# A fused LayerNorm, mLSTM and spiking-FFN kernel: linked small normalisation steps split up, fewer of them, and new instruction orders

## What is computed

```python
q = layernorm(x)
ig, fg = gates(q, c, c)                      # 8 input and 8 forget gates per token
D = exp(cumsum(log_sigmoid(fg)) differences + ig - row maximum), lower triangle
C = (q k^T / sqrt(32)) * D
h = C / (max(|C.sum(-1)|, exp(-rowmax)) + 1e-6) @ v
x1 = x + tanh(g_xattn) * layernorm(h) * ln_scale
y = square(relu(layernorm(x1) @ W_fc^T)) @ W_proj^T
out = x1 + tanh(g_ffn) * (spikes of 5 integrate-and-fire steps driven by y) / 5
```

## Time and profile before

| | |
|---|---|
| median of 3 runs | 615.34 us (615.02 to 616.83) |
| profiled execution, span | 615.3 us |
| TensorE busy | 571.4 us (93%), 6032 matmuls |
| VectorE | 526.3 us (86%), 1291 instructions |
| GpSimd | 493.3 us (80%) |
| ScalarE | 485.8 us (79%) |
| mean granted TensorE clock | 0.980 |

### The profile page before, as it was taken

How to read it: one execution, slowest core, us unless ns; L and a number is a source line. 1 busy time by engine, 2 the same in 40 slices (tenths; PEclk the granted TensorE clock), 3 DMA queues, 4 the chain that set the end, 5 groups by cost and what they waited for, 6 DMA issues and landing times.

```text
span 615.3 us, 17747 instructions
## 1 busy us (share of the span) xinstructions
PE 571.4 (93%) x6032; PEld 479.2 (78%) x6032; DVE 526.3 (86%) x1291; ACT 485.8 (79%) x1011; POOL 493.3 (80%) x541
## 2 busy tenths in 40 slices
PE   0568988999999999999999999999999999999995
PEld 0357888887888888888788888888888888887894
DVE  4789889989989898989989898989999888878446
ACT  3776878897888888888888788888888777776673
POOL 4878889996997889887997889887997887955542
PEclk9995989999999999999999999999999999999998
DMA  8775736664664637662663637752675427401002
GB/s 271 168 145 115 160 74 124 168 139 95 124 149 96 155 84 127 171 146 70 123 163 83 158 83 131 187 126 70 121 167 130 87 48 148 121 4 35 0 2 70
DMA packets 73193, 71.34 MB, mean 116 GB/s; under 512 B 8720, under 2 KB 68752, under 8 KB 73104
## 3 DMA queue, kind: packets, MB, share of 16 engines
q1 hardware_dynamic: 71888, 70.00, 50.5%
q10 hardware_dynamic: 1216, 0.21, 0.2%
HBM read 27.44 MB, written 8.39 MB: 58 GB/s over the span
## 4 chain that ended last, share of the span: by engine, by line
PE 82%; SPq 7%; DMA 3%; ACT 2%; issue 2%; DVE 2%; POOL 1%; ACTq 0%; POOLq 0%; DVEq 0%
PE z_ps L1069 28%; PE y_ps L1135 26%; PE qk_ps L773 4%; PE arg_ps L758 4%; PE misc_ps L503 4%; SPq L706 3%; PE misc_ps L569 2%; SPq L553 2%; PE pv_ps L822 2%; PE pv_ps L820 2%; PE pv_ps L821 2%; PE pv_ps L897 2%; DMA x<-w_proj_t 2%; PE y_ps L1164 1%; PE arg_ps L1135 1%
## 5 line engine op out<-in xcount | busy, mean ns | idle before, releaser
L802 POOL TENSOR_TENSOR c_lo<-decay 128x512 bf16<-128x512 f32 x128 | 132.7, 1043 | 31.9 <-DVE decay L792 31.8
L1112 POOL TENSOR_TENSOR sq_lo<-w_raw,sq_hi 128x512 fp32r<-128x512 f32 (+1 forms) x96 | 111.8, 1166 | 39.6 <-ACT w_raw L1092 39.3
L1069 PE MATMUL z_ps<-x_hi,wfc_hi 128*128 128x512 f32 (+1 forms) x288 | 114.4, 397 | 1.8 <-ACT w_raw L1079 1.8
L1069 PE MATMUL z_ps<-x_hi,wfc_lo 128*128 128x512 f32 (+1 forms) x288 | 106.1, 368 | 0.0
L1069 PE MATMUL z_ps<-x_lo,wfc_hi 128*128 128x512 f32 (+1 forms) x288 | 105.9, 368 | 0.0
L1135 PE MATMUL y_ps<-sq_hi,wpr_hi 128*128 128x512 f32 (+1 forms) x256 | 103.8, 406 | 0.0
L1135 PE MATMUL y_ps<-sq_hi,wpr_lo 128*128 128x512 f32 (+1 forms) x256 | 97.4, 380 | 0.0
L1135 PE MATMUL y_ps<-sq_lo,wpr_hi 128*128 128x512 f32 (+1 forms) x256 | 97.1, 379 | 0.0
L792 DVE TENSOR_TENSOR decay<-qk_ps,decay 128x512 f32<-128x512 f32 x128 | 87.0, 680 | 9.4 <-ACT decay L784 6.5
L784 ACT ACTIVATE decay<-arg_ps,lqk_col 128x512 f32<-128x512 f32 x128 | 86.6, 677 | 10.5 <-PE arg_ps L761 9.5
L1153 DVE SCALAR_TENSOR_TENSOR spikes<-y_ps,spikes 128x1024 bf16<-128x1024 f32 (+1 forms) x64 | 73.8, 1153 | 1.2
(11 more groups left out here) (193 smaller groups left out, 1727.8 us busy)
## 6 DMA issues: line engine op xcount, KB each, us to landing
x_in<-x SPq DMA_DIRECT2D x32, 256.0 KB, 3.2
kT_in<-ctx_cols SPq DMA_DIRECT2D x32, 256.0 KB, 3.2
v_in<-ctx_rows SPq DMA_DIRECT2D x32, 256.0 KB, 4.3
k_stack<-kT_hi SPq DMA_DIRECT2D x64, 128.0 KB, 3.2
k_stack<-kT_lo SPq DMA_DIRECT2D x64, 128.0 KB, 3.7
q_stack<-qT_hi SPq DMA_DIRECT2D x64, 128.0 KB, 4.1
q_stack<-qT_lo SPq DMA_DIRECT2D x64, 128.0 KB, 4.3
out<-w_raw SPq DMA_DIRECT2D x32, 256.0 KB, 3.4
```

What stands on the lines that cost most here:

```text
L802: e.tensor_tensor(c_lo[i % NCH][:, :], c, top(c), ALU.subtract).then_inc(sem("c_lo"), 1)
L1069: ins = e.matmul(z_ps[:, tokens(q)], lhsT, rhs, start=(n == 0), stop=(n == len(terms) - 1))
L1112: e.tensor_tensor(sq_lo[n % NSQ][:, tokens(q)], relu[n % NRE][:, tokens(q)], sq_hi[n % NSQ][:, tokens(q)].bitcast(fp32), ALU.subtract).the ...
```

## The change

It splits the tied steps into separate ones with semaphores of their own: `ln1_stats` into `ln1_bn` and `ln1_stats`, `ln1_rstd` into `ln1_log` and `ln1_rstd`, the same for ln2 and ln3, `h_norm` into `h_scale`, `h_add`, `h_abs`, `h_denom`, `h_recip` and `h_norm`, `x1_step` into `x1_scale` and `x1_step`, `square` into `sq_hi_step` and `square`. The normaliser was three VectorE operations and is now one on ScalarE (`h_abs`) and one on VectorE; the epsilon goes into the floor once per gate group (`floor_eps`, on GpSimd). Batches 0 and 1 get statistics, `Ln` and `Exp` each for itself, and VectorE applies them in one operation per 128 tokens. The gate weights come in an arrangement of one run of 384 bytes per partition, where 64-byte pieces were fetched. All five lists are new, and written out without loops.

```diff
+    LN1 = [(0, 1), (1, 1)] + [(b, 2) for b in range(2, B, 2)]
+    FIRST = 2
...
-            for dst, src in ((gw_raw[:, :, :], gate_w.rearrange("(c p) g -> p c g", p=P)), (gate_bias[:, :], gate_b)):
+            for dst, src in ((gw_raw[:, :, :], gate_w), (gate_bias[:, :], gate_b)):
...
-        def rstd_of(e, rstd, lnv, mv):
-
-            link(e, "scalar", e.activation(lnv[:, :], mv[:, :, 1], ACT.Ln, bias=eps_col[:, :]))
-            return e.activation(rstd[:, :], lnv[:, :], ACT.Exp, scale=-0.5)
...
+            n = LN1[i][1] * ST
+            e.activation(lnv1[:, 0:n], mv1[i % 2][:, 0:n, 1], ACT.Ln, bias=eps_col[:, :]).then_inc(sem("ln1_log"), 1)
...
+            e.activation(rstd1[i % 2][:, 0:n], lnv1[:, 0:n], ACT.Exp, scale=-0.5).then_inc(sem("ln1_rstd"), 1)
...
+        def ln1_first(e, b):
+
+            e.wait_ge(sem("ln1_rstd"), b + 1)
+            for t in range(ST):
+                dst, src = xln_views(b, t)
+                ins = e.tensor_scalar(dst, src, mv1[b % 2][:, t, 0:1], rstd1[b % 2][:, t:t + 1], ALU.subtract, ALU.mult)
+            ins.then_inc(sem("xln_first"), 1)
...
+        def floor_eps(e, g):
...
+            e.tensor_scalar(least, least, EPS, None, ALU.add).then_inc(sem("floor_eps"), 1)
...
-            link(e, "vector", e.scalar_tensor_tensor(most[:, :, :], row_sum, -1.0, least, ALU.mult, ALU.max))
-            link(e, "vector", e.tensor_tensor(denom, row_sum, most[:, :, :], ALU.max))
-            link(e, "vector", e.tensor_scalar(denom, denom, EPS, None, ALU.add))
-            link(e, "vector", e.reciprocal(rdenom[:, :, :], denom))
...
+            e.activation(most[:, :, :], pv_heads[:, :, :, DH], ACT.Abs).then_inc(sem("h_abs"), 1)
...
+            e.wait_ge(sem("h_abs"), b + 1)
...
+            e.scalar_tensor_tensor(denom, most[:, :, :], EPS, floor[g % 3][:, 0:ST, row:row + NH],
+                                   ALU.add, ALU.max).then_inc(sem("h_denom"), 1)
...
-            link(e, "scalar", e.activation(sq_hi[n % NSQ][:, tokens(q)], r, ACT.Square))
+            e.activation(sq_hi[n % NSQ][:, tokens(q)], relu[n % NRE][:, tokens(q)], ACT.Square).then_inc(sem("sq_hi"), 1)
```

More of the change, by code:

```diff
@@ L206, in misc_order @@
         def misc_order():
[L208 to L218, removed]
+            return [("q", 0), ("g", 0), ("q", 1), ("gT", 0), ("q", 2), ("g", 1), ("fT", 0), ("gT", 1), ("q", 3),
[13 rows of a table added]
         MISC_ORDER = misc_order()
@@ L1366, in scalar_program @@
             am_split(e, 2, 0)
+            gates_out(e, 4)
+            h_abs(e, 0)
             decay_exp(e, 1, 0)
@@ new lines, in scalar_program @@
+            decay_exp(e, 9, 0)
+            ln1_apply(e, 13)
+            square(e, 3, 3)
+            square(e, 3, 4)
+            gates_out(e, 12)
+            ln3_log(e, 7)
+            decay_exp(e, 9, 1)
+            ln3_rstd(e, 7)
+            sq_hi_step(e, 3, 5)
+            square(e, 3, 5)
+            relu_step(e, 3, 6)
+            h_abs(e, 8)
+            decay_exp(e, 9, 2)
+            q_hi(e, 13)
+            sq_hi_step(e, 3, 6)
+            ln3_apply(e, 7)
+            ln2_log(e, 8)
@@ new lines, in scalar_program @@
+            ln2_rstd(e, 9)
+            relu_step(e, 4, 4)
+            sq_hi_step(e, 4, 4)
+            gates_out(e, 14)
+            ln3_log(e, 9)
+            decay_exp(e, 11, 0)
+            relu_step(e, 4, 5)
+            square(e, 4, 3)
+            q_hi(e, 15)
+            ln3_rstd(e, 9)
+            sq_hi_step(e, 4, 5)
+            square(e, 4, 4)
+            square(e, 4, 5)
+            gates_out(e, 15)
+            h_abs(e, 10)
+            ln3_apply(e, 9)
+            relu_step(e, 4, 6)
@@ new lines, in scalar_program @@
+            gates_out(e, 16)
+            ln3_log(e, 11)
+            h_abs(e, 12)
+            ln3_rstd(e, 11)
+            relu_step(e, 5, 6)
+            decay_exp(e, 13, 2)
+            ln3_apply(e, 11)
+            q_hi(e, 17)
+            ln2_log(e, 12)
+            decay_exp(e, 13, 3)
+            ln2_rstd(e, 12)
+            relu_step(e, 5, 7)
+            sq_hi_step(e, 5, 6)
+            sq_hi_step(e, 5, 7)
+            square(e, 5, 6)
+            square(e, 5, 7)
+            gates_out(e, 17)
@@ new lines, in scalar_program @@
+            square(e, 7, 3)
+            relu_step(e, 7, 5)
+            decay_exp(e, 16, 3)
+            sq_hi_step(e, 7, 5)
+            square(e, 7, 4)
+            q_hi(e, 20)
+            ln3_log(e, 15)
+            ln3_rstd(e, 15)
+            decay_exp(e, 17, 0)
+            ln1_apply(e, 21)
+            square(e, 7, 5)
+            decay_exp(e, 17, 1)
+            relu_step(e, 7, 6)
+            h_abs(e, 16)
+            gates_out(e, 20)
+            ln3_apply(e, 15)
+            q_hi(e, 21)
@@ new lines, in scalar_program @@
+            ln2_log(e, 17)
+            sq_hi_step(e, 8, 3)
+            ln2_rstd(e, 17)
+            relu_step(e, 8, 4)
+            ln1_apply(e, 23)
+            square(e, 8, 3)
+            ln3_log(e, 17)
+            ln3_rstd(e, 17)
+            decay_exp(e, 19, 0)
+            gates_out(e, 22)
+            sq_hi_step(e, 8, 4)
+            q_hi(e, 23)
+            relu_step(e, 8, 5)
+            sq_hi_step(e, 8, 5)
+            square(e, 8, 4)
+            gates_out(e, 23)
+            h_abs(e, 18)
```

3430 lines of the change are left out of this document (2633 added, 797 removed), and 13 rows, old and new, of the table SLOTS.

## The result

The changed kernel takes **642.11 us** (median of 4 runs, 640.23 to 644.03) against 615.18 us of the kernel before in the same session: a ratio of **1.0419**, 95% interval 1.0383 to 1.0455. It is slower by 27 us in the medians, where 612.4 us was forecast. The profiled execution took 640.23 us, its span 638.4.

What follows compares the result with a forecast made beforehand. TensorE, busy 498.16 of 500 us from 100 to 600 us, was taken as the bound. The span 615.3, less 3.8 at the start, plus 0.9 at the end and 0 in the steady part, gave 612.4 us; range 606.3 to 617.3.

Steps and rivals of the forecast that it cites:

- The steady part: nothing.: From 100 to 600 us: 0.43 us of VectorE freed per batch about cancels against waiting for ScalarE's Abs; 0 us.
- The start, -3.8 us: Ramp to about 100 us: q_hi(0) at 14.3, 2.8 us earlier, softplus of batch 0 3.8 earlier, bounds 1.4 and 4.7.
- The 1.0 us for `split_wpr_hi(0)`: In the start: this step leaves the stretch between gates_out(0) and the softplus, worth 1.0 us more.
- lower bound of 608.8: Low end of the sum's own range, 615.3 - 4.7 - 1.8; its high end was 615.2.
- The end, +0.9: Last 10 us: count_T(16) ahead of job 17's last slice makes its spikes 1.2 us later; net 0.9, bounds 0 and 1.3.
- The ramp closes as well: Rival, 45 to 100 us: denser work keeps TensorE's clock up, at most 6.1 us more gained, 606.3 us; 20%.
- Slower by VectorE waiting for ScalarE: Rival, steady part: the h_abs round trip exceeds VectorE's free 2 us per batch, starving TensorE by 16 us: 628 us; 5%.
- The gain is taken back: Rival, before 100 us: GpSimd order, keys, masks or clock swallow the start's gain, leaving the end: 616.2 us; 16%.
- Slower by the table loads: Rival, start: each of four ScalarE table loads on the path costs 1.2 us more, 4.9 in all: 617.3 us; 7%.

Runs made afterwards that it cites:

- e8: e5 with every tile at the SBUF address it has in the kernel before: 617.92 us, ratio 1.0015.
- e13: e1 with the tiles at the addresses of the kernel before: 628.19 us, ratio 1.0212.
- e11: The whole changed kernel with every tile back at its old address: 637.78 us, ratio 1.0340.
- e1: Changed kernel with two VectorE normaliser operations, one operand of each in PSUM, in place of the round trip through ScalarE: 629.79 us, ratio 1.0207.
- e5: Changed operations with the normaliser of e1, in the five engines' orders of the kernel before: 619.85 us, ratio 1.0054.
- e6: e5 with the changed orders up to batch 6 and the old orders from there on: 620.51 us, ratio 1.0060.
- e10: e6 with every tile at its address in the kernel before: 617.59 us, ratio 1.0005.
- e2: Changed kernel with ScalarE's Abs written to PSUM, so that h_denom reads PSUM and SBUF; round trip kept: 633.34 us, ratio 1.0258.
- e9: Kernel before with gw_sum made a piece of kw, all tiles declared behind it 256 bytes lower, no instruction changed: 618.17 us, ratio 1.0001.
- e3: Kernel before with the third small normaliser operation reading two SBUF operands, same values and operation count: 625.14 us, ratio 1.0124.
- e12: e9 with an unused filler of 128 bytes ahead of x1ln: 619.95 us, ratio 1.0069.
- e14: e9 with an unused filler of 192 bytes ahead of x1ln: 620.38 us, ratio 1.0087.
- e15: e9 with an unused filler of 64 bytes ahead of x1ln: 617.78 us, ratio 0.9996.
- e16: e9 with an unused filler of 128 bytes ahead of gw_hi: 616.86 us, ratio 0.9979.
- e7: e5 with the normaliser as changed (round trip through ScalarE, h_denom with two SBUF operands), in the old orders: 668.62 us, ratio 1.0851.
- e4: e1 with x2_lo_step moved ahead of the gate chain in five of the six groups of the steady part: 640.61 us, ratio 1.0400.

## Why the prediction was wrong

The chain e8, e13, e11, changed kernel adds one part at a time, and its ratios give the loss in parts: **new lists 12.1 us** (1.0212 - 1.0015), **normaliser 7.9** (1.0340 - 1.0212; 13.0 between e1 and the changed kernel, at the shifted addresses), **addresses 4.9** (1.0419 - 1.0340; 1.6 to 4.3 in the medians of the pairs e1 and e13, e5 and e8, e6 and e10, changed kernel and e11), all else 0.9 with an interval that holds zero. That is 25.8 us, the ratio's 0.0419; the medians give 27. Each difference is uncertain by 2 to 3 us, and the normaliser's and the addresses' shares depend on which is taken away first.

*The failed step: "The steady part: nothing."* It has three faults.
- `h_denom` was costed at 0.21 us, the start-to-start time of the old small operations, and the 0.43 us saved was set against the wait for ScalarE. Those rows were the wrong neighbours: each of the old operations has an operand in PSUM, `h_denom` reads `most` and `floor`, both in SBUF. It measured 0.734 us in the mean, so the three operations that took 0.64 us were not undercut at all. The prediction asked neither where the operands lie nor what GpSimd does meanwhile, and in the traces the duration goes with both: 1.26 us beside a `sq_lo`, 0.184 us with GpSimd idle (at 210 us), never over 0.183 us in e2. One operation of GpSimd is not the limit: the 2.849 us lie across four of them.
- The step took for granted that work moved to another place in a list keeps its duration. The gate chain's did not (`row_max` 0.41 to 1.33 us), because before it ran where GpSimd happened to wait.
- That 63.5 us of free VectorE time "hide" a change is an average. TensorE has 1.84 us of slack in 500, so a late `x_lo`, `cmul` or state product shows as its idle time (13.9 us in 500).

Nothing was said of addresses; the change's diff shows the tiles that moved them.

*The start, -3.8 us.* Its times came true (14.30, 18.70), its baseline did not. In the profile of before the second x landed only at 9.29. In e9, whose program starts with the same instructions, the timelines of VectorE and ScalarE show:

```profile
6.38 0.75 DVE L396 BATCH_NORM_STATS2 stat<-x_in 128x6 f32<-128x256 f32 x2
...
14.36 0.60 ACT L526 ACTIVATE qT_hi<-misc_ps 128x512 bf16<-128x512 f32 x1 [1.27 <-PE misc_ps L503]
```

In e3, e12, e14, e15 and e16 the second x is there by 6.6 as well, and `q_hi(0)` starts between 14.2 and 15.7, the softplus between 19.7 and 22.1. Of the 2.8 us at least half were one late transfer in one execution. The 1.0 us for `split_wpr_hi(0)` held: from `q_hi(0)` to the softplus 4.4 us pass now, 5.4 before and 5.5 to 6.4 in all these. So the changed start is worth 1.0 to 3.4 us at the softplus, 0.7 us at job 2 (e10 against e8) and nothing that can be told from noise at the end. The prediction asked what the changed kernel would do if the second x came late, not what the kernel before does when it comes in time. Its lower bound of 608.8 also takes off 1.8 us for which it names no term.

*The end, +0.9.* The order is as described, the size was about half. Counted from the end of slice 6 of job 17 (606.28 before, 628.89 now), the last slice starts 0.5 us later (0.92 against 0.39 us behind it), the spikes of job 17 start 0.5 later (1.91 against 1.40), not 1.2, and the program ends 0.5 later (9.53 against 9.01). The other runs agree: 8.99 to 9.04 us with the old lists' end (e3, e5, e8, e9, e10, e16), 9.40 to 9.55 with the new (e1, e11, e13).

*The rivals.* "The ramp closes as well" did not come: the clock is granted sooner (0.69 against 0.50 from 45 to 62 us, 1.00 against 0.95 from 62 to 100; at 0.50 from 42.0 to 55.7 us where it was from 45.0 to 62.0), but TensorE has 7.9 us idle from 62 to 100 us where it had 4.1, and the lead of 2.4 us at job 0 is a lag of 0.8 at job 2. In e13, without the round trip, it has 4.7 us idle there. "Slower by VectorE waiting for ScalarE" named the right place and the wrong price: the wait is 9.0 us of VectorE in all and costs some 3 us (e2 against e1). e7, which also has the SBUF operand, lies 49 us above e5, so the price could have been far higher. "The gain is taken back" can't be judged: against before with its x in time there was little to take back (e10 and e8). "Slower by the table loads" is refuted: 0.03 us behind a load, where 1.2 was the price. As for the splitting itself, e8, which has it together with the other changed operations, measures 1.0015 with the interval at 229.5 ns; TensorE would hide a gain of VectorE too, so what the 0.1 us of a link is worth is not shown.

What stays open: which single waits make up the 12 us of the new lists. From 100 to 600 us TensorE stands idle for more than 0.15 us in 23 places of the changed kernel, 13.2 us in all, against 3 places and 1.4 us before, and 14 places and 8.7 us in e13. The two `z` waits behind the gate chain are 4.0 of the 13.2 and 4.3 of the 8.7 us; the others are not explained, and e4 shows that the obvious repair makes new ones.

## What to carry to other kernels

Price a VectorE operation by where its operands lie: a neighbour of the same size with one operand in PSUM told nothing about one with two in SBUF (0.18 against 0.734 us in the mean), which with GpSimd at work lasted as long as the rest of GpSimd's current operation, 1.26 us beside a `sq_lo`, and in three of 32 places longer, up to 2.849 us. Before trusting a term that rests on one execution's landing of a transfer, ask what both kernels do when it lands in time. When tiles are added or removed, compare two builds at equal addresses, or the tiles' places become part of what is measured (4.9 us here).

## What the runs showed of the hardware

- A 128x16 operation of VectorE with two SBUF operands took from 0.175 to 2.849 us, and one with an operand in PSUM 0.172 to 0.183 us, at the same places in the program. In 30 of 32 places the first overlapped GpSimd and ended within 0.06 us of the end of one of its operations, in three of these not of the first. In e1 GpSimd's `sq_lo` grew too, from 1.29 to as much as 1.73 us, where it met the 32x256 operations of the gate chain with two SBUF operands.
- One-operand operations are hit as well: `TENSOR_SCALAR` of 32x128 from SBUF to SBUF took from 0.27 to 1.31 us. In the changed kernel the 1.31 us lie beside a `sq_lo` of 1.37 us, and end within 0.08 us of its end.
- The distance between the tiles ahead of `x1ln`, the weights among them, and those from there on, the streamed operand among them, changes the pace of 512-column fp32 matmuls: 229.4 to 229.6 ns where it is as before or all tiles moved together, 230.2, 232.5 and 233.2 ns where it changed by 64, 128 and 192 bytes, worth up to 0.9% of the time in the kernel before (e14). Which pair of tiles it is, and the mechanism, are open.
- Around waits of TensorE of 3.54 and 3.67 us (e4) its granted clock lay at 0.51 and 0.50 for 6.9 and 6.8 us; at a wait of 2.59 us in the changed kernel it stayed at 1.00.
